# Local attention with scores, transposes and values at the head of a slot; shifted values by transfers; value bias added at the output

## The chip, the core and the metric

The kernel runs on one core of a Trainium2 chip as one program of 63,082 instructions. The core has TensorE (PE, matrix products, and PEld, its weight loads), VectorE (DVE), ScalarE (ACT), GpSimd (POOL) and SyncE (SP), which here only issues transfers. Each engine runs its own instructions in the order in which they were written and waits on semaphores for the others. The metric is the device time of one execution in microseconds; less is better.

## The reference, cut to what matters

A chain of eleven kinds of layer acts on a residual stream of 2048 tokens by 128 channels. Three of them are touched.

```python
# _L1_ffn_ref: two layers, called twice in the network; WINDOW = 64, HEADS = 8, DIM_HEAD = 64, n = 1024, b = 2
def _layer(x, wqkv, qs, ksc, wo, lg, lb, w1, b1, w2, b2):
    q, k, v = jnp.split(shift_token(x) @ wqkv, 3, axis=-1)      # then split into heads
    q, k = rotary_xpos(l2norm(q) * qs, l2norm(k) * ksc)
    o = local_attention(q, k, v)
    x = x + o @ wo
    h = layernorm(shift_token(x)) * lg + lb
    a, g = jnp.split(h @ w1 + b1, 2, axis=-1)
    return x + (a * jax.nn.gelu(g, approximate=False)) @ w2 + b2

def local_attention(q, k, v):            # a window sees itself and the window before
    bk, bv = look_around(bk), look_around(bv)
    sim = jnp.einsum('bhwid,bhwjd->bhwij', bq, bk)
    mask = (i < j) | (i > j + WINDOW) | (j == -1)
    attn = jax.nn.softmax(jnp.where(mask, -jnp.finfo(sim.dtype).max, sim), axis=-1)
    return jnp.einsum('bhwij,bhwjd->bhwid', attn, bv)

# _L1_attn_b_ref (16 heads) and _L2_attn_a_ref (one head, causal)
v = x @ Wv.T + bv
probs = softmax(scores)                  # every row of it sums to 1
out = probs @ v
return out @ Wo.T + bo
```

## The kernel before

`PLAN` lists the stages; `L1f0` and `L1f1` are the two layers of the local-attention block and are run as one stage, twice in the program. Channels lie on the partitions, tokens along the free axis. `PS` is PSUM, eight banks of 128x512; `AR` is the working memory, `WS` the weights, `TP` eight slots of 128x512, `VXT` the shifted values.

**The stage of local attention** (`l1f_pe`, `l1f_act`, `l1f_dve`, `l1f_pool`, `l1f_sp`) is written as a row of 158 slots. The work is cut into 8 groups (a quarter of the tokens in one of the two layers) and each group into 16 units: one pair of heads and 128 queries, that is two windows. Unit `u` is spread over slots: its scores stand in TensorE's slot `u`, the masked maximum (L1986) and the bias for the exponential in VectorE's slot `u`, the two exponentials (L1922) in ScalarE's slot `u`, the reciprocal of the sums (L1994) in VectorE's slot `u+1`, the normalising multiply (L2068) in GpSimd's slot `u+1`. The transposes of the probabilities (L1897) stand in TensorE's slot `u+2`, VectorE's copy of the transposed tile out of PSUM (L2040) too, and the products with the values (L1851, L1853) in TensorE's slot `u+4`. After four units ScalarE copies the output bank 3 (`copy(e, OB[:, r, :], bank(3))`, L518).

Around that, a table (`l1f_dense`) deals the dense work of the next group and of the layer's second half to the slots: `a` (a projection of q or k, read by VectorE for the cosine half, by ScalarE for the raw copy that is swapped), `norm`, `v`, `wide`, `wo`, `ln`, `gate`, `up`, `down`. A slot has a list `first` and a list `second` of them. A dense product of 128x512 in f32 shows as two MATMUL records. TensorE's slot before is: scores, values, `first`, transposes, `second`. VectorE's slot is: masked maximum, bias, reciprocal, dense work of earlier slots, gating of `first`, copy of the transposed tile, gating of `second`, shifted values. Scores have a single pair of banks, so the scores of slot `u+1` wait for the masked maximum of `u`; the transposed tile has a single bank too.

**Shifted values** (`VX`, tile VXT). A window's lower half of keys is its own, the upper half is the window before. So for each of the four tiles of 128 tokens in a group VectorE copies partitions 0 to 63 of that tile (L2047) and 64 to 127 of the tile before (L2049), in slots 1 to 4 of the group.

**SP's queue in this stage** (`l1f_sp`, L2104): the rotary part needs halves of 32 partitions swapped; eight times a group, four transfers of 32x512 go from `RAW` to `TP`. The weights of the stage after next are loaded ahead of the swaps of group 7.

**Value projections.** In `attn16_pe` (stages `L0b`, `L1b`, `L3f`) and in `l2a_pe` (stage `L2a`) 16 products of 128x128 make the values. In `L1b` and `L2a` each is followed by a product with one row of ones and one row of bias (`PS<-WS,CS`, 1x128). The scores' operands of the 16-head stages are brought into place by transfers, 12 of them issued by ScalarE (L1114).

Of the kernel before, what the change touches and what calls it, by code (L numbers as in the profile page):

```python
# [121 lines left out]
def layout(sec, i):  # L122
# [52 lines left out]
    if sec in ("L1b", "L2a"):  # L175
# [3 lines left out]
                ("wo", 128, lambda: i[p + "Wo"].T), ("bv", 128, lambda: rows(i[p + "bv"][None, :])),  # L179
                ("bq", 1, lambda: col(i[p + "bq"][o])), ("bk", 1, lambda: col(i[p + "bk"][o])), ("bo", 1, lambda: col(i[p + "bo"]))]  # L180
# [77 lines left out]
LINES = ("w_in0", "w_in1", "swap_in0", "swap_in1", "swap_in2", "swap_in3", "qk_in0", "qk_in1", "qk_in2", "qk_first", "pad_in", "x_in", "consts_in", "out_done")  # L258
# [190 lines left out]
def program(nc, plan, wall, half, pad, xin, out):  # L449
    where, _ = places(plan)  # L450
    ctx = ExitStack()
    with ctx:
# [20 lines left out]
        swap_in = [F.swap_in0, F.swap_in1, F.swap_in2, F.swap_in3]  # L473
        qk_in = [F.qk_in0, F.qk_in1, F.qk_in2]
# [595 lines left out]
        def ring(k):  # L1070
            return k % 3
# [142 lines left out]
        def attention_act(e, w, s, scale, causal):  # L1214
            units = units_of[causal]
            for kind, n, *args in order[causal]:
# [28 lines left out]
                if kind == "turn":  # L1245
                    c = args[0]
                    w.wait_ge(*F.at_turned.on((s, c)))
                    copy(e, ATTT[:, cs(c)], bank(ring(n))).then_inc(*F.at_out.up((s, c)))
# [80 lines left out]
        def project_v_pe(e, w, s, n, ready, W, bname, heads, banks):  # L1329
            for i in range(16):  # L1330
# [3 lines left out]
                more = [(C("ONE")[0:1, :], W(bname)[0:1, :])] if bname else []  # L1334
                mm(e, bank(b, 8 * heads), (n[:, ts_(i)], W("wv")), *more).then_inc(*F.v_mm.up((s, i)))
# [25 lines left out]
        def l0b_pe(e, w, s, W):  # L1361
# [11 lines left out]
            project_v_pe(e, w, s, n, normal(s), W, None, 4, OWN8)  # L1373
            attention_pe(e, w, s, V4, lambda h: 9 * (h // 4), False, W("wo"), x_added(s))

        def l0b_act(e, w, s, W):
# [5 lines left out]
            attention_act(e, w, s, float(np.float32(128.0) ** np.float32(-0.5)), False)  # L1382
# [29 lines left out]
        def attn16_pe(e, w, s, W, n, ready, causal, bv, added):  # L1412
# [6 lines left out]
            project_v_pe(e, w, s, n, ready, W, bv, 16, OWN8)  # L1419
            attention_pe(e, w, s, V16, lambda h: 9 * h, causal, W("wo"), added)  # L1420

        def attn16_act(e, w, s, W, causal, biased):
# [5 lines left out]
            attention_act(e, w, s, float(8.0 ** -0.5), causal)  # L1428
# [16 lines left out]
        def l1b_pe(e, w, s, W):  # L1445
            attn16_pe(e, w, s, W, big(0), normal(s), False, "bv", x_added(s))
# [320 lines left out]
        def l1f_pe(e, w, s, W0):  # L1767
# [94 lines left out]
            for u in SLOTS:  # L1862
# [16 lines left out]
                if 0 <= u - 4 < UNITS:  # L1879
                    g, r, i = unit(u - 4)  # L1880
                    w.wait_ge(*F.win_pt.on((s, u - 4)))
                    if i == 0:
                        w.wait_ge(*F.head_v_copied.on((s, g, 3)))
                        w.wait_ge(*free[3])
# [1199 lines left out]
```

## Time and profile before

| | |
|---|---|
| three runs | 4466.93, 4472.2, 4471.73 us; median 4471.73 |
| profiled execution | 4480.15 us, span 4478.3 us |
| PE busy | 3922.5 us, 88% of the span |
| DVE busy | 3042.6 us, 68% |
| ACT busy | 2359.4 us, 53% |
| POOL busy | 1224.9 us, 27% |
| mean granted clock of TensorE | 0.909 of 2.4 GHz |

The span goes from the first to the last instruction. Busy shares are averages over the whole program and say little about one stage. "Idle before, releaser" is the time in which an engine stood still ahead of an instruction, and the instruction that released it. The view of waits sums that by pairs: who waited for whom. The chain of waits goes back from the last instruction, at each step to what released it.

### The profile page before, as it was taken

What the parts mean: (1) busy time and instruction counts of PE and PEld (TensorE: products, weight loads), DVE (VectorE), ACT (ScalarE), POOL (GpSimd) and SP (SyncE); (2) the same over time, 40 slices, a digit from 0 to 9 for tenths busy, and PEclk for the clock granted to TensorE, in tenths of its full rate; (3) what the DMA queues carried; (4) which work ended last, traced back from release to release, by engine and by line L of the source; (5) the groups of instructions that cost most, each with busy time, mean ns of one, the idle gap of its engine ahead of it and who ended that gap; (6) DMA issues with size and microseconds to landing.
All of it is one profiled execution on the core that took longest, in us unless ns stands there. A gap on an engine that the chain in (4) does not pass through costs nothing.

```text
span 4478.3 us, 63082 instructions
## 1 busy us (share of the span) xinstructions
PE 3922.5 (88%) x22638; PEld 1897.2 (42%) x22640; DVE 3042.6 (68%) x7970; ACT 2359.4 (53%) x4061; POOL 1224.9 (27%) x1835
## 2 busy tenths in 40 slices
PE   8899968998899988898886778899998999969999
PEld 5222345555432235555552324555554334433343
DVE  4899566878589968877345994566666883278732
ACT  3477644555447765555345553445443673326732
POOL 1100023333220013333112663111113233442334
PEclk8799978889879998988797998899997999979999
DMA  1100002111020011111000000000010100011000
GB/s 55 26 18 16 15 34 72 39 34 42 6 61 20 16 49 43 35 38 28 5 7 5 1 0 9 10 16 17 9 40 20 30 16 1 0 51 28 16 1 10
DMA packets 48336, 104.86 MB, mean 23 GB/s; under 512 B 15220, under 2 KB 15220, under 8 KB 46744
## 3 DMA queue, kind: packets, MB, share of 16 engines
q1 hardware_dynamic: 46872, 99.26, 8.1%
q8 instruction: 179, 2.93, 0.3%
q10 hardware_dynamic: 1152, 1.57, 0.2%
q14 instruction: 133, 1.09, 0.1%
HBM read 41.01 MB, written 1.05 MB: 9 GB/s over the span
## 4 chain that ended last, share of the span: by engine, by line
PE 54%; DVE 29%; ACT 7%; POOL 4%; issue 4%; DMA 1%; ACTq 1%; SPq 0%; POOLq 0%; DVEq 0%
PE PS L511 32%; DVE SM L1274 7%; PE PS L1184 7%; PE PS L1136 5%; PE PS L2743 3%; DVE AR L2547 3%; DVE AR L515 2%; PE PS L1166 2%; DVE AR L1986 1%; PE PS L538 1%; ACT PS L2491 1%; POOL SV L608 1%; ACT AR L518 1%; DVE TP L515 1%; DVE AR L596 1%
## 5 line engine op out<-in xcount | busy, mean ns | idle before, releaser
L511 PE MATMUL PS<-AR,WS 128*128 128x512 f32 (+1 forms) x2112 | 1068.8, 646 | 78.1 <-DVE AR L515 29.6
L1236 ACT ACTIVATE AR<-PS 128x1024 f32<-128x1024 f32 (+3 forms) x896 | 788.9, 931 | 206.0 <-PE PS L1166 201.7
L1274 DVE TENSOR_REDUCE SM<-PS 128x1 f32<-128x512 f32 x1280 | 803.7, 684 | 71.3 <-PE PS L1136 70.3
L518 ACT ACTIVATE AR<-PS 128x512 f32<-128x512 f32 (+6 forms) x600 | 368.7, 623 | 533.9 <-PE PS L511 410.1
L511 PEld LDWEIGHTS PS<-AR,WS 128*128 128x128 f32 (+1 forms) x2112 | 407.9, 204 | 546.8 <-issue 415.4
L1136 PE MATMUL PS<-AR 51*128 51x512 bf16 (+3 forms) x1792 | 508.2, 384 | 61.1 <-DVE SM L1274 16.2
L1184 PE MATMUL PS<-AR 128*32 128x512 f32 (+3 forms) x3584 | 447.6, 572 | 2.5 <-POOL AR L1326 1.9
L1922 ACT ACTIVATE AR<-AR,SM 128x128 f32<-128x128 f32 x512 | 248.3, 486 | 362.3 <-DVE SM L515 360.5
L1136 PEld LDWEIGHTS PS<-AR 51*128 51x128 bf16 x1792 | 133.2, 94 | 597.1 <-DVE SM L1274 407.4
L511 PE MATMUL PS<-AR,H 115*115 115x128 bf16 (+3 forms) x912 | 212.3, 311 | 104.4 <-DVE TP L2550 37.5
L2068 POOL TENSOR_TENSOR AR<-AR,SM 128x256 f32<-128x256 f32 x256 | 162.9, 636 | 486.9 <-DVE SM L1994 473.4
L1166 PE MATMUL PS<-AR 51*128 51x512 bf16 (+3 forms) x1792 | 288.7, 366 | 8.3 <-ACT AR L1236 5.3
L2817 DVE TENSOR_TENSOR AR<-AR,PS 128x512 f32<-128x512 f32 x128 | 87.5, 688 | 256.7 <-PE PS L511 256.7
L1312 POOL CAST MBT<-SM 128x8 bf16<-128x8 f32 x128 | 28.2, 221 | 840.6 <-DVE SM L1277 699.3
L606 POOL TENSOR_SCALAR SV<-LNS 128x4 f32<-128x4 f32 x148 | 28.8, 195 | 834.8 <-DVE LNS L589 563.8
L1271 DVE CUSTOM_DVE_ANT_0 TP<-PS,H 128x384 f32<-128x384 f32 (+3 forms) x512 | 226.3, 487 | 41.3 <-PE PS L1136 35.8
L515 DVE SCALAR_TENSOR_TENSOR AR<-PS,WS,AR 128x512 f32<-128x512 f32 x148 | 109.7, 748 | 186.2 <-PE PS L511 155.6
L511 PE MATMUL PS<-AR 128*128 128x16 f32 (+3 forms) x920 | 198.0, 366 | 27.9 <-DVE AR L913 10.9
L2831 POOL TENSOR_TENSOR AR<-AR 128x512 f32<-128x512 f32 x128 | 159.4, 1268 | 228.8 <-ACT AR L518 228.8
L511 PE MATMUL PS<-WS,AR 128*128 128x256 f32 (+4 forms) x640 | 205.6, 456 | 15.3 <-DVE TP L515 6.0
L511 PEld LDWEIGHTS PS<-AR,H 115*115 115x115 bf16 (+3 forms) x912 | 98.9, 121 | 272.4 <-DVE TP L2550 60.7
L2075 POOL TENSOR_TENSOR AR<-AR,TP 128x512 f32<-128x512 f32 x128 | 162.2, 1267 | 142.5 <-DVE TP L515 142.5
(320 smaller groups left out, 6969.4 us busy)
## 6 DMA issues: line engine op xcount, KB each, us to landing
TP<-RAW SPq DMA_DIRECT2D x512, 64.0 KB, 2.0
AR<-AR SPq DMA_DIRECT2D x720, 32.0 KB
WS<-wall SPq DMA_DIRECT2D x4, 3654.5 KB, 11.2
WS<-wall SPq DMA_DIRECT2D x8, 902.5 KB, 4.5
WS<-wall SPq DMA_DIRECT2D x2, 3334.5 KB, 11.0
WS<-wall SPq DMA_DIRECT2D x1, 2384.0 KB, 9.1
WS<-wall SPq DMA_DIRECT2D x1, 1543.5 KB, 6.2
AR<-AR ACTq DMA_DIRECT2D x48, 32.0 KB
```

The lines of the kernel that those rows point to most:

```text
L511: t = e.matmul(o, l, r, start=(n == 0), stop=(n == len(pairs) - 1))
L515: return e.scalar_tensor_tensor(out=o, in0=a, scalar=s, in1=b, op0=f1, op1=f2)
L518: return e.activation(o, i, ACT.Copy, scale=1.0)
L1136: e.matmul(bank(p, m), l, r, start=True, stop=True).then_inc(*F.at_scores_max.up((s, k, i, rr, k0, g)))
L1166: t = e.matmul(sv[:, g, off:512], l, r, start=True, stop=True)
L1184: t = e.matmul(bank(7)[32 * j:32 * j + 32, t0:t1], V[:, 8 * b + kti, v0:v0 + 32], pv[:, j % 2, t0:t1], start=(kti == 0), stop=(kti == nk - 1))
L1236: e.activation(pv[:, :, off:512], sv[:, :, off:512], ACT.Exp, scale=scale).then_inc(*F.at_exp.up((s, u, p2)))
L1271: e.tensor_tensor_reduce(out=slot(5 + len(masked) % 3, m), in0=bank(ring(n + g), m), in1=H["MASKED"][:, 512 - m:512], scale=1.0, scalar=-3 ...
L1274: e.tensor_reduce(top, bank(ring(n + g), m), AX.X, ALU.max).then_inc(*F.at_max.up((s, k, i, rr, k0, g)))
L1922: t = e.activation(pw[:, z, :], pw[:, z, :], ACT.Exp, bias=nm[:, 2 + z:3 + z], scale=rq[:, z:z + 1], accum_out=nm[:, 4 + z:5 + z])
L2068: e.tensor_tensor(pw, pw, nm[:, 4:6].unsqueeze(2).to_broadcast([128, 2, 128]), ALU.mult).then_inc(*F.win_p.up((s, u - 1)))
L2075: e.tensor_tensor(d, d, slot(4 + j % 4), ALU.add).then_inc(*F.head_sum.up((s, g, j)))
```

## The change

1. In TensorE's slot the transposes move from behind `first` to right behind the scores, ahead of the values. Both dense lists follow.
2. In VectorE's slot the copy of the transposed tile moves to right behind the bias, ahead of the reciprocal.
3. In ScalarE's slot the copy of the output bank moves ahead of the exponentials.
4. The shifted values are no longer copied by VectorE but transferred, by SP, with four semaphores of their own. In SP's queue the swaps of a group now go one group ahead, and the transfers of shifted values stand between the first four of them.
5. In `L1b` and `L2a` the bias of the values is not multiplied into every value but added when the attention's output is copied out of PSUM (the weights of a row sum to 1). The bias is kept as one column instead of 128.

```diff
@@ l1f_pe
                     scores(u).then_inc(*F.win_score.up((s, u)))
+                if 0 <= u - 2 < UNITS:
+                    w.wait_ge(*F.win_p.on((s, u - 2)))
+                    w.wait_ge(*(F.win_pt.on((s, u - 3)) if u >= 3 else free[2]))
+                    for g in range(2):
+                        t = e.transpose(TURNED[:, g, :], pw[:, g, :], C("I"))
+                    t.then_inc(*F.win_turned.up((s, u - 2)))
                 if 0 <= u - 4 < UNITS:
                     w.wait_ge(*F.win_pt.on((s, u - 4)))
-                    w.wait_ge(*F.win_vx.on((s, g, i)))
+                    w.wait_ge(*vx_in[i].on((s, g, i)))
                     values(u - 4).then_inc(*F.win_pv.up((s, u - 4)))
                 dense(first)
-                if 0 <= u - 2 < UNITS:
...
                 dense(second)
@@ l1f_act
+                if 0 <= u - 4 < UNITS and u % 4 == 3:
+                    w.wait_ge(*F.win_pv.on((s, u - 4)))
+                    copy(e, OB[:, r, :], bank(3)).then_inc(*F.win_o.up((s, g, r)))
                 if 0 <= u < UNITS:
                     for z in range(2):
                         t = e.activation(pw[:, z, :], pw[:, z, :], ACT.Exp, bias=nm[:, 2 + z:3 + z], scale=rq[:, z:z + 1], accum_out=nm[:, 4 + z:5 + z])
-                if 0 <= u - 4 < UNITS and u % 4 == 3:
...
@@ l1f_dve
                     stt(e, nm[:, 2:4], nm[:, 0:2], -1.0, rq, ALU.mult, ALU.mult).then_inc(*F.win_bias.up((s, u)))
+                if 0 <= u - 2 < UNITS:
+                    w.wait_ge(*F.win_turned.on((s, u - 2)))
+                    e.tensor_copy(PTR[(u - 2) % 3], TURNED).then_inc(*F.win_pt.up((s, u - 2)))
...
-                if 0 <= u < UNITS and 1 <= u % 16 <= 4:
-                    t = e.tensor_copy(VX[0:64, i, :], VH[0:64, 4 * (g % 2) + i, :])
-                    if i or g % 2:
-                        t = e.tensor_copy(VX[64:128, i, :], VH[64:128, 4 * (g % 2) + i - 1, :])
@@ l1f_sp
+            def shifted_values(g, i):
+                w.wait_ge(*F.head_v_copied.on((s, g, 3)))
+                if g:
+                    w.wait_ge(*F.win_pv.on((s, 16 * g - 4 + i)))
+                e.dma_start(VX[0:64, i, :], VH[0:64, 4 * (g % 2) + i, :]).then_inc(*vx_in[i].up((s, g, i), 16))
+                if i or g % 2:
+                    last = (4 * (g % 2) + i - 1) % 8
+                    e.dma_start(VX[64:128, i, :], VH[64:128, last, :]).then_inc(*vx_in[i].up((s, g, i), 16))
+            for j in range(8):
+                swap(0, j)
             for g in range(8):
-                if g == 7:
+                if g == 6:
                     load(e, s + 2)
                 for j in range(8):
+                    if j < 4:
+                        shifted_values(g, j)
+                    if g < 7:
+                        swap(g + 1, j)
@@ project_v_pe, and alike in l2a_pe
-                more = [(C("ONE")[0:1, :], W(bname)[0:1, :])] if bname else []
-                mm(e, bank(b, 8 * heads), (n[:, ts_(i)], W("wv")), *more).then_inc(*F.v_mm.up((s, i)))
+                mm(e, bank(b, 8 * heads), (n[:, ts_(i)], W("wv"))).then_inc(*F.v_mm.up((s, i)))
@@ attention_act (bv is 0.0 where a stage has no bias), and alike in l2a_act
-                    copy(e, ATTT[:, cs(c)], bank(ring(n))).then_inc(*F.at_out.up((s, c)))
+                    e.activation(ATTT[:, cs(c)], bank(ring(n)), ACT.Identity, bias=bv).then_inc(*F.at_out.up((s, c)))
```

TensorE, first pass of local attention, slot 2 of the third group. L1838, L1840 and L1842 are the scores, L1851 and L1853 the values, L1897 the transposes, L511 dense work. Before:

```order
L1838 MATMUL PS<-AR 64x64 [waits win_dve]
L1838 MATMUL PS<-AR 64x64
L1840 MATMUL PS<-AR 64x128 x2
L1842 MATMUL PS<-AR 64x64 x2
L1851 MATMUL PS<-AR 64x64 x2
L1853 MATMUL PS<-AR,VXT 64x64 x2
L511 MATMUL PS<-AR,WS 128x512 [waits head_act]
L1897 MATMUL PS<-CS,AR 128x128 [waits win_dve,win_pool]
L1897 MATMUL PS<-CS,AR 128x128
L511 MATMUL PS<-CS,TP 128x2 [waits ln_act,head_act]
L511 MATMUL PS<-CS,TP 128x2 x3
```

After (L1884 are the transposes, L512 the dense work):

```order
L1838 MATMUL PS<-AR 64x64 [waits win_dve]
L1838 MATMUL PS<-AR 64x64
L1840 MATMUL PS<-AR 64x128 x2
L1842 MATMUL PS<-AR 64x64 x2
L1884 MATMUL PS<-CS,AR 128x128 [waits win_dve,win_pool]
L1884 MATMUL PS<-CS,AR 128x128
L1851 MATMUL PS<-AR 64x64 x2
L1853 MATMUL PS<-AR,VXT 64x64 x2
L512 MATMUL PS<-AR,WS 128x512 [waits head_act]
L512 MATMUL PS<-CS,TP 128x2 [waits ln_act,head_act]
L512 MATMUL PS<-CS,TP 128x2 x3
```

The transposes and their wait for VectorE and GpSimd have moved ahead of the values and of the 128x512 product; nothing stands between the two dense lists any more.

VectorE, slot 2 of the same group. L1986 is the masked maximum, L515 with SM the bias, L1994 the reciprocal, L2040 the copy of the transposed tile, L2047 and L2049 the shifted values. Before:

```order
L1986 ISA AR,SM<-PS,H 128x128 [waits win_pe]
L1986 ISA SM 128x1
L1986 ISA AR,SM<-PS,H 128x128
L1986 ISA SM 128x1
L515 SCALAR_TENSOR_TENSOR SM<-SM 128x2 [waits win_dve]
L1994 RECIPROCAL SM<-SM 128x2 [waits win_act]
L515 SCALAR_TENSOR_TENSOR AR<-PS,WS 128x512 [waits head_act]
L515 SCALAR_TENSOR_TENSOR TP<-TP,WS 128x512 [waits swap_in0]
L2040 COPY AR<-PS 128x256 [waits win_pe]
L2047 COPY VXT<-AR 64x512
L2049 COPY VXT<-AR 64x512
```

After (L1995 is the copy of the transposed tile, L1999 the reciprocal, L516 the rest):

```order
L1986 ISA AR,SM<-PS,H 128x128 [waits win_pe]
L1986 ISA SM 128x1
L1986 ISA AR,SM<-PS,H 128x128
L1986 ISA SM 128x1
L516 SCALAR_TENSOR_TENSOR SM<-SM 128x2 [waits win_dve]
L1995 COPY AR<-PS 128x256 [waits win_pe]
L1999 RECIPROCAL SM<-SM 128x2 [waits win_act]
L516 SCALAR_TENSOR_TENSOR AR<-PS,WS 128x512 [waits head_act]
L516 SCALAR_TENSOR_TENSOR TP<-TP,WS 128x512 [waits swap_in0]
```

The copy, with its wait for TensorE, stands ahead of the reciprocal and of the dense work; both copies into VXT are gone.

SP, the first slots of the second group of the first pass, after. L2090 is a swap, L2096 and L2099 are the shifted values:

```order
L2096 DMA VXT<-AR 64x512 [waits win_pe,head_act]
L2099 DMA VXT<-AR 64x512
L2090 DMA TP<-RAW 32x512 [waits head_pool,head_act]
L2090 DMA TP<-RAW 32x512 x3
L2096 DMA VXT<-AR 64x512 [waits win_pe]
L2099 DMA VXT<-AR 64x512
L2090 DMA TP<-RAW 32x512 [waits head_pool,head_act]
L2090 DMA TP<-RAW 32x512 x3
```

Before, the swaps stood alone there. Now a wait for TensorE's values (win_pe) stands ahead of each of the first four swaps.

## Rows read from the trace of the kernel before

**Rows 1.** The page, the chain that ended last, by engine.

```profile
PE 54%; DVE 29%; ACT 7%; POOL 4%; issue 4%; DMA 1%; ACTq 1%; SPq 0%; POOLq 0%; DVEq 0%
```

**Rows 2.** Busy times in both passes: us, busy (records) by engine, clock, DMA, GB/s.

```profile
737.00:1215.00 478.00, 425.06 (x3740) 255.64 (x3738) 365.96 (x1425) 264.61 (x744) 164.66 (x205) 0.89 0.14 33
1693.00:2165.00 472.00, 414.19 (x3722) 251.04 (x3721) 362.87 (x1413) 262.35 (x741) 164.06 (x204) 0.89 0.14 33
```

**Rows 3.** TensorE's waits, first pass: who for whom, total us, times, longest.

```profile
PE PS L1851 <- ACT AR L518: 13.5, 12, 2.0
PE PS L1838 <- DVE SM L1986: 12.8, 22, 1.5
PE PS L1897 <- DVE AR L2040: 8.3, 14, 1.1
```

**Rows 4.** TensorE's waits, second pass.

```profile
PE PS L1851 <- ACT AR L518: 15.7, 16, 2.0
PE PS L1897 <- DVE AR L2040: 15.1, 22, 2.9
PE PS L1838 <- DVE SM L1986: 10.2, 19, 0.7
```

**Rows 5.** Groups by line: busy us, mean ns, idle before and its releasers.

```profile
L2040 DVE COPY AR<-PS 128x256 f32<-128x256 f32 x256 | 106.7, 417 | 84.3 <-PE PS L1897 83.7
...
L1897 PEld LDWEIGHTS PS<-CS,AR 128*128 128x128 f32 x512 | 66.0, 150 | 127.8 <-issue 105.6 <-POOL AR L2068 17.7
...
L2047 DVE COPY VXT<-AR 64x512 f32<-64x512 f32 x64 | 57.4, 898 | 0.0
```

**Rows 6.** Timeline 900.9 to 901.4, TensorE: start us, length us, line, shapes, records.

```profile
901.03 0.20 PEld L1897 LDWEIGHTS PS<-CS,AR 128*128 128x128 f32 x2
901.03 0.44 PE L1897 MATMUL PS<-CS,AR 128*128 128x128 f32 x2
```

**Rows 7.** Timeline 908 to 911, all engines.

```profile
908.18 0.38 PE L1897 MATMUL PS<-CS,AR 128*128 128x128 f32 x2
...
908.50 0.27 PE L1838 MATMUL PS<-AR 64*64 64x64 f32 x2
...
908.72 0.23 PE L1842 MATMUL PS<-AR 64*64 64x64 f32 x2
...
908.87 0.34 PE L1851 MATMUL PS<-AR 128*64 128x64 f32 x4
908.94 0.41 DVE L2047 COPY VXT<-AR 64x512 f32<-64x512 f32 x1
...
909.79 0.14 PEld L1897 LDWEIGHTS PS<-CS,AR 128*128 128x128 f32 x1 [0.24 <-issue]
909.82 0.29 DVE L1986 CUSTOM_DVE_ANT_0 AR<-PS,H 128x128 f32<-128x128 f32 x1
...
910.22 0.38 PE L1897 MATMUL PS<-CS,AR 128*128 128x128 f32 x2
...
910.44 0.73 PE L511 MATMUL PS<-CS,TP 128*128 128x2 f32 x6
...
910.68 0.61 POOL L2068 TENSOR_TENSOR AR<-AR,SM 128x256 f32<-128x256 f32 x1 [2.53 <-DVE SM L1994]
```

**Rows 8.** SP's issues of the swaps by source line.

```profile
L2104 SPq DMA_DIRECT2D TP<-RAW x512: 507/591/2063, 704.3 to 2090.2; - x171
...
DMA to landing us min/median/max: 1.9/2.0/3.8
```

**Rows 9.** Value projections: the one-row products by line.

```profile
L511 PE MATMUL PS<-WS,CS 1*128 1x128 f32 x64 | 22.4, 444 | 0.0
```

**Rows 10.** Timeline at the end of the value projection, 16 heads, TensorE.

```profile
1267.26 1.03 PE L1136 MATMUL PS<-AR 51*128 51x512 bf16 x3
```

**Rows 11.** Timeline of ScalarE's transfers there.

```profile
1249.30 9.09 ACTq L1114 DMA_DIRECT2D AR<-AR  x12
```

**Rows 12.** Timeline at the first score of the single-head stage.

```profile
2222.89 0.80 PE L2135 MATMUL PS<-AR 128*128 128x128 f32 x2 [0.37 <-ACT AR L518]
```

More of the change, by code:

```diff
@@ L1410, in program, with attn16_pe @@
         SIDES = [("wq", "bq", QP), ("wk", "bk", KP)]
-        def attn16_pe(e, w, s, W, n, ready, causal, bv, added):
+        def attn16_pe(e, w, s, W, n, ready, causal, added):
             for j in range(8):
@@ L1445, in l1b_pe @@
         def l1b_pe(e, w, s, W):
[L1446 removed]
+            attn16_pe(e, w, s, W, big(0), normal(s), False, x_added(s))
         def l1b_act(e, w, s, W):
@@ L1898, in l1f_pe @@
                     t.then_inc(*F.win_turned.up((s, u - 2)))
+                if 0 <= u - 4 < UNITS:
+                    g, r, i = unit(u - 4)
+                    w.wait_ge(*F.win_pt.on((s, u - 4)))
+                    if i == 0:
+                        w.wait_ge(*F.head_v_copied.on((s, g, 3)))
+                        w.wait_ge(*free[3])
+                    w.wait_ge(*vx_in[i].on((s, g, i)))
+                    values(u - 4).then_inc(*F.win_pv.up((s, u - 4)))
+                if 0 <= u - 4 < UNITS:
+                    g, r, i = unit(u - 4)
+                    if i == 3:
+                        free[3] = F.win_o.on((s, g, r))
+                dense(first)
                 if u == -2:
@@ L2092, in l1f_sp, with swap @@
         def l1f_sp(e, w, s):
+            def swap(g, j):
+                done, into = swap_in[j % 4], slot(4 + j % 4)
+                w.wait_ge(*F.head_raw.on((s, g, j)))
+                if 8 * g + j >= 4:
+                    w.wait_ge(*F.head_sum.on((s, g, j - 4) if j >= 4 else (s, g - 1, j + 4)))
+                for p in range(4):
+                    e.dma_start(into[32 * p:32 * p + 32, :], RAW[j % 2][32 * (p ^ 1):32 * (p ^ 1) + 32, :]).then_inc(*done.up((s, g, j), 16))
+            def shifted_values(g, i):
+                w.wait_ge(*F.head_v_copied.on((s, g, 3)))
+                if g:
[6 more added lines that the diff above has]
+                swap(0, j)
             for g in range(8):
-                if g == 7:
+                if g == 6:
                     for c in ALL:
@@ L2183, in l2a_act @@
                     w.wait_ge(*F.one_pv.on((s, u - 2)))
-                    copy(e, n[:, ts_(8 * b + i)], bank(6 + u % 2, 128)).then_inc(*F.one_out.up((s, u - 2)))
+                    e.activation(n[:, ts_(8 * b + i)], bank(6 + u % 2, 128), ACT.Identity, bias=W("bv")).then_inc(*F.one_out.up((s, u - 2)))
         def l2a_dve(e, w, s, W):
```

62 lines of the change are left out of this document (18 added, 44 removed).

## The prediction

> **What bounds the kernel now.** I read the chain of waits first: TensorE holds 54% of the span, VectorE 29%, ScalarE 7% [rows 1]. So no engine alone sets the end; the loop through several of them does in places. The change sits in two stages, local attention (which the plan runs twice) and the two value projections with a bias, so the busy times of the local-attention passes come next: 478 and 472 us long, TensorE busy 425.1 and 414.2, VectorE 366.0 and 362.9, granted clock 0.89 in both [rows 2]. TensorE sits idle for 53 + 58 = 111 us in them, and that is the most that any reordering of waits can give back. Who ends those waits is in the view of waits. In the first pass: values waiting for ScalarE's copy of the output bank 13.5 us, scores waiting for VectorE's masked maximum 12.8, transposes waiting for VectorE's copy of the transposed tile 8.3 [rows 3]. In the second: 15.7, 10.2 and 15.1 [rows 4]. Together 29.2 for the output bank, 23.0 for the maximum, 23.4 for the transposed copy: 75.6 of the 111 us.
>
> VectorE is late for two visible reasons. It shifts the values itself, 57.4 us in 64 copies of the lower half and 56 more of the upper half, and in the slot shown a pair of them, begun at 908.94, stands ahead of the masked maximum that begins at 909.82, though the scores had ended at 908.72 + 0.23 = 908.95 [rows 5, 7]. And it stands idle 84.3 us ahead of the copy of the transposed tile, 83.7 of them for TensorE, because the transposes come behind a dense product [rows 5].
>
> **The change, part by part.** My profiled execution took 4480.15 us (span 4478.3), the median shown is 4471.73; I work on the profiled one and move the difference to the median.
>
> *Waits of TensorE that go.* With ScalarE's output copy ahead of its exponentials, the bank is asked for a slot later than it is freed: the 29.2 us go. With VectorE's copy at the head of its slot, transposes no longer meet it: the 23.4 go. Of the 23.0 for the maximum I take 16: VectorE loses the shifting copies (57.4 and, at this slot's 0.41 for each of the 56 others, 23, so 80 us) and most of 84 us idle, against 729 busy [rows 2, 5, 7]; what stays late are slots in which its own dense work is long. Sum -69. Bounds: -52 if the maximum's waits all stay, -76 if all three go. What is late next is the product chain of TensorE itself.
>
> *What the head order costs TensorE.* Today a pair of transposes between two dense products costs 0.22 us (start 910.22 to the next start 910.44), and its weight load runs from 909.79 under the product before it. Behind the scores it has no such cover: where transposes follow the small value products, load and product start together at 901.03, and the pair takes 0.44 instead of 0.38 us; where scores follow transposes, 908.18 to 908.50, it is 0.32 [rows 6, 7]. From scores to values is 0.15 today (908.72 to 908.87). The new head has two such changes of tile where there was one: 0.15 + 0.32 against 0.15 + 0.22 at least, so +0.10, and +0.2 if the step behind the scores is as long as the longer ones. I take 0.15 in each of the 256 slots, +38 us (26 to 51). This is TensorE's own time, nothing hides it where TensorE is the bound. The Trainium skill ("TensorE: Matmul & The Clock Gate", section "Step-by-step: what each phase is for") says that TensorE pulls weight loads ahead of matmuls in flight, when row groups don't conflict or the load goes to the background buffer. By that rule a load is free behind a long product, and there the trace agrees (0.43 us ahead in 909.79 to 910.22); if it held behind the scores too the term would be near 0 and the sum 38 us lower, but the 901.03 rows show no lead.
>
> *A new wait.* The transposes now stand at the head of TensorE's queue behind their wait for the probabilities, and values and dense products behind them. The normalising multiply on GpSimd ends 1.47 us after the masked maximum begins (909.82 to 910.68 + 0.61); VectorE's copy of the transposed tile now stands between, +0.42, so 1.89. A slot with one dense product and nothing more lasts 0.37 (908.50 to 908.87) + 1.35 (values and product, to 910.22) + 0.32 (transposes, as above) = 2.04 us [rows 7]. From scores ended at 0.45 in one slot, the probabilities are ready at 0.45 + 0.08 + 1.89 = 2.42; the transposes want them at 2.04 + 0.37 = 2.41, or 0.15 later with the dearer head. So on time they cost nothing, and each microsecond by which VectorE is late in a short slot is paid on TensorE. Even now 17.7 us of weight loads of transposes wait for GpSimd, with a product ahead of most [rows 5]. Bounds: 0, and 17.7 plus one product of 0.96 for about as many loads as there are short slots in which VectorE's own dense work is longest (two in 16, so 32): 48. I take 15, nearer to the low end since VectorE sheds over 100 us; that is one late microsecond per 16 slots.
>
> *Shifted values by transfer.* 120 more issues in SP's queue. One swap issue takes 591 ns in the median, and landing 2.0 us [rows 8]. In four slots of every 16 SP now issues 2 + 4 = 6 transfers, 3.5 us, in slots of 2 to 3.5 us, so it falls behind by a few us, and the fifth slot has no issue and holds the output projection, four products. The shifted values are wanted four slots after they are issued. I take 0; if the swaps' readers on VectorE do wait, up to 2.4 us (one swap) in each of 16 groups, +38. The early load of the next stage's weights stands where it stood, between the swaps of group 6 and those of group 7.
>
> *Bias out of the value projection.* 64 records of one-row products, 22.4 us busy, half in each of two stages [rows 9]. In the 16-head attention the last pair of them stands right ahead of the scores, which start at 1267.26. Without them the scores are held by the transfers that ScalarE issues until 1249.30 + 9.09 = 1258.39 and their landing 2.0 later, so they can start at 1260.4: -6.9 us [rows 8, 10, 11]. In the single-head stage the first score starts at 2222.89, 0.37 us after TensorE ran out of work, held by the copy of the last product; nothing else is in the way, so half of the busy time, 11.2, less what overlaps, -10.4 [rows 12]. Bounds for both together: -14 and -20. ScalarE's copies of the attention's output become copies with a bias, 16 wide ones and 16 narrow ones; no row separates what that adds, I take +1.5 us for the 32 (0 to 3, a tenth of a microsecond each at most where nothing hides it). The weights that shrink by 127 columns load long before they are used: 0.
>
> Sum: -69 + 38 + 15 + 0 - 17.3 + 1.5 = -32, that is 4448 for the profiled execution and 4439 against the median of 4471.73.
>
> **Rivals** (times against the median of 4471.73). (1) *The loop was the bound.* VectorE sheds 80 us of copies and 84 us of idling, and if the remaining waits of TensorE fall with it (the 111 us down to some 15) and transposes are never late: -96 + 38 - 16 = -74, 4398. For it: 29% of the chain on VectorE [rows 1]. Against it: TensorE is already busy 88% of the passes.
> (2) *Local attention gives nothing.* The new wait and the switches eat the 69: -16 from the bias alone, 4456. For it: 38 + 31 is inside the bounds above.
> (3) *Slower.* VectorE now waits for the transposes with its reciprocal, sines, norms and gating behind, the transposes wait for GpSimd, and GpSimd for that reciprocal one slot earlier. Each late slot is then handed on instead of being absorbed behind the first dense product. If half of the 256 slots are late by one product's worth, 0.96 us: +123 - 69 + 38 - 16 = +76, 4548; at 0.6 us +40, 4512. It decides from 47 us of new waits on. Against it: the one-product slot just meets, and by the table that places the dense work only four or five slots in 16 are that short.
> (4) *SP's queue.* Swaps late by one swap in each group: -32 + 38 = +6, 4478. For it: the four issues of a swap alone fill 2.4 us of a slot [rows 8]. Against it: the wide fifth slot.
>
> **How the numbers follow.** About 0.2% of the median, 9 us, is what a measurement can tell. Forecast 0.46 (own range 4422 to 4455), rival 1 0.18, rival 2 0.17, rival 3 0.13, rival 4 0.06. Faster by over 0.2% (below 4463): the forecast but for 0.02, rival 1, and half of rival 2, 0.71. Within: the rest of rival 2 and most of rival 4, 0.15. Slower: 0.14. The range that leaves two in ten outside reaches from 4402, into rival 1, to 4480, past rivals 2 and 4; rival 3 stays out. The granted clock of 0.89 in the passes is left where it is: fewer gaps may raise it, and more short products at the head may lower it; both ends are inside the range.
>
> **What would show it.** Waits of values for ScalarE's copy and of transposes for VectorE's copy near 0; VectorE's idle time ahead of that copy far under 84 us; a wait of the transposes on GpSimd that stands on TensorE itself, about 15 us in both passes; 0.3 us between transposes and values in each slot; scores of the 16-head stage held by a transfer; passes shorter by 8 us each. The prediction is wrong if that GpSimd wait passes 47 us, if VectorE waits for swaps by more than 20 us, or if TensorE's idle time in the passes falls below 30 us.

## The result and the profile after

| | before | after |
|---|---|---|
| median of the timed runs, us | 4471.97 (4466.93 to 4476.41, 4 runs) | 4451.24 (4446.88 to 4454.48, 4 runs) |
| ratio after/before, 95% interval | | 0.9953 [0.9936, 0.9971] |
| profiled execution, us (its span) | 4480.15 (4478.3) | 4450.58 (4448.7) |

The change gains 21 us by the medians and 30 between the two profiled executions. The prediction said 4439, with a range of 4402 to 4480. The time lies in the forecast's own range (4422 to 4455), but the traces tell a different story from the one forecast: nearly all of the gain comes from the bias, and local attention gave back what it won.

The page after has the chain that ended last by engine [rows 1]: VectorE's share went down by three points and TensorE's went up by as many.

```profile
PE 57%; DVE 26%; ACT 6%; POOL 5%; issue 4%; SPq 1%; DMA 1%; ACTq 0%; POOLq 0%; DVEq 0%
```

From mark to mark, after against before: each pass of local attention from its first scores to its last values, +2.8 and -5.5 us; from there to the first score of the 16-head stage -6.4, of the single-head stage -18.6; everything else together -1.9. Sum -29.6, the difference of the spans.

Busy times in both passes, after. The columns are those of rows 2, but the windows here end with the last values of a pass:

```profile
736.00:1202.00 466.00, 432.37 (x3709) 253.36 (x3710) 337.93 (x1350) 264.85 (x740) 164.33 (x204) 0.86 0.22 50
1688.00:2147.00 459.00, 429.84 (x3711) 253.43 (x3710) 338.19 (x1350) 264.64 (x740) 164.35 (x204) 0.86 0.22 51
```

The same stretches before (in rows 2 some us more stood behind the last values):

```profile
738.00:1200.00 462.00, 410.12 (x3708) 249.22 (x3700) 360.59 (x1410) 260.30 (x739) 164.58 (x204) 0.89 0.15 34
1693.00:2157.00 464.00, 406.68 (x3710) 247.72 (x3708) 361.75 (x1411) 260.14 (x739) 164.06 (x204) 0.90 0.14 34
```

926 us became 925. TensorE's idle time fell as meant, from 109.2 to 62.8 us. Its busy time rose by the same amount, from 816.8 to 862.2, for the same number of products. And the granted clock fell from 0.89 to 0.86.

TensorE's waits after, first pass [rows 3] and second pass [rows 4]:

```profile
PE PS L1884 <- POOL AR L2059: 22.5, 32, 1.6
PE PS L1838 <- DVE SM L1986: 7.3, 14, 0.8
...
PE PS L1884 <- POOL AR L2059: 19.6, 29, 1.6
PE PS L1838 <- DVE SM L1986: 6.2, 11, 0.8
```

The waits for the output copy (29.2) and the transposed copy (23.4) are gone, as forecast. 13.5 of 23.0 us for the masked maximum stay, and transposes now wait 42.1 us for GpSimd's multiply.

One slot of TensorE after, at the full clock (start, length): scores, transposes, values [rows 7].

```profile
968.69 0.23 PE L1842 MATMUL PS<-AR 64*64 64x64 f32 x2
968.85 0.44 PE L1884 MATMUL PS<-CS,AR 128*128 128x128 f32 x2
969.22 0.34 PE L1851 MATMUL PS<-AR 128*64 128x64 f32 x4
```

The transposes take 0.37 us from start to start of what follows, where they took 0.22 between dense products.

VectorE's side, after: its copy by line [rows 5], and its waits in the first pass.

```profile
L1995 DVE COPY AR<-PS x256: 410/417/425, 740.6 to 2143.6; 128x256 f32<-128x256 f32 x128
its engine sat idle before it (us, times) until:
  PE PS L1884: 4.2, 12
```

```profile
DVE AR L1986 <- PE PS L1842: 64.3, 58, 5.2
DVE AR L516 <- PE PS L512: 26.7, 16, 3.8
DVE TP L516 <- DMA TP<-RAW: 15.4, 16, 2.1
```

84.3 us of idling ahead of the copy became 4.2, but VectorE now idles 64.3 us in this pass (66.3 in the second) for scores: it is the follower. It waits 15.4 + 14.7 us for swaps, against 3.5 + 7.4 before.

The start of the 16-head scores [rows 10] and the value projection of the single-head stage with its first score [rows 12], after:

```profile
1261.97 0.97 PE L1137 MATMUL PS<-AR 51*128 51x512 bf16 x3 [2.85 <-DMA AR<-AR]
...
2189.59 3.73 PE L512 MATMUL PS<-WS,AR 128*128 128x128 f32 x32
2193.69 0.49 PE L2143 MATMUL PS<-AR 128*128 128x128 f32 x2 [0.37 <-ACT AR L519]
```

### The profile page after: what moved, and what is told of

It reads as the page before. It is cut to its first block, busy times and chain, and to the rows that moved or that the text cites. A ratio compares the mean times of both kernels' runs of the same rounds, so it can differ in the third digit from the quotient of the medians.

```text
span 4448.7 us, 62998 instructions
## 1 busy us (share of the span) xinstructions
PE 3930.3 (88%) x22576; PEld 1885.0 (42%) x22576; DVE 2994.7 (67%) x7850; ACT 2368.0 (53%) x4061; POOL 1223.3 (27%) x1835
## 4 chain that ended last, share of the span: by engine, by line
PE 57%; DVE 26%; ACT 6%; POOL 5%; issue 4%; SPq 1%; DMA 1%; ACTq 0%; POOLq 0%; DVEq 0%
PE PS L512 32%; DVE SM L1275 7%; PE PS L1185 7%; PE PS L1137 5%; DVE AR L2555 3%; PE PS L2751 3%; DVE AR L516 2%; PE PS L1167 2%; PE PS L1884 2%; PE PS L539 1%; ACT PS L2499 1%; POOL SV L609 1%; DVE SV L516 1%; PE PS L1851 1%; DVE AR L1986 1%
## 5 line engine op out<-in xcount | busy, mean ns | idle before, releaser
L512 PE MATMUL PS<-AR,WS 128*128 128x512 f32 (+1 forms) x2112 | 1062.3, 643 | 68.4 <-DVE AR L516 26.1
L519 ACT ACTIVATE AR<-PS 128x512 f32<-128x512 f32 (+6 forms) x568 | 358.9, 637 | 571.7 <-PE PS L512 403.0
L512 PEld LDWEIGHTS PS<-AR,WS 128*128 128x128 f32 (+1 forms) x2112 | 405.6, 203 | 524.3 <-issue 411.9
L1137 PE MATMUL PS<-AR 51*128 51x512 bf16 (+3 forms) x1792 | 507.1, 382 | 63.6 <-DVE SM L1275 16.2
L512 PE MATMUL PS<-AR,H 115*115 115x128 bf16 (+3 forms) x912 | 208.4, 310 | 104.3 <-DVE TP L2558 37.5
L516 DVE SCALAR_TENSOR_TENSOR AR<-PS,WS,AR 128x512 f32<-128x512 f32 x148 | 109.7, 748 | 198.0 <-PE PS L512 181.4
L512 PE MATMUL PS<-WS,AR 128*128 128x256 f32 (+4 forms) x640 | 207.6, 466 | 18.6 <-DVE TP L516 8.6
L512 PE MATMUL PS<-AR 128*128 128x16 f32 (+3 forms) x920 | 193.0, 360 | 27.9 <-DVE AR L914 10.9
L1986 DVE CUSTOM_DVE_ANT_0 AR<-PS,H 128x128 f32<-128x128 f32 x512 | 127.7, 287 | 133.1 <-PE PS L1842 130.6
L512 PEld LDWEIGHTS PS<-AR,H 115*115 115x115 bf16 (+3 forms) x912 | 97.8, 121 | 268.8 <-DVE TP L2558 60.7
## 6 DMA issues: line engine op xcount, KB each, us to landing
WS<-wall SPq DMA_DIRECT2D x2, 3334.5 KB, 10.4
```

Of the source, the lines that this page charges most:

```text
L512: t = e.matmul(o, l, r, start=(n == 0), stop=(n == len(pairs) - 1))
L516: return e.scalar_tensor_tensor(out=o, in0=a, scalar=s, in1=b, op0=f1, op1=f2)
L519: return e.activation(o, i, ACT.Copy, scale=1.0)
L1137: e.matmul(bank(p, m), l, r, start=True, stop=True).then_inc(*F.at_scores_max.up((s, k, i, rr, k0, g)))
L1986: t = e.tensor_tensor_reduce(out=PW[u % 4][:, z, :], in0=bank(z, 128), in1=H["BAND0" if top(u) else "BAND"], scale=1.0, scalar=-3.0e38, op ...
```

## The experiments

The parts are numbered as in the change: 1 TensorE's order, 2 VectorE's order, 3 ScalarE's copy, 4 shifted values, 5 bias. Each ratio is to the kernel before, run on the same chip.

| run | parts | median us | ratio, 95% interval |
|---|---|---|---|
| e1 | 5 | 4452.10 | 0.9945 [0.9930, 0.9960] |
| e2 | 1 2 3 4 | 4469.27 | 0.9989 [0.9974, 1.0003] |
| e3 | none, bias products of 128 rows | 4454.31 | 0.9950 [0.9938, 0.9962] |
| e4 | 3 | 4442.83 | 0.9918 [0.9905, 0.9932] |
| e5 | 4 | 4431.12 | 0.9907 [0.9890, 0.9924] |
| e6 | 1 2 | 4476.41 | 1.0012 [0.9996, 1.0029] |
| e7 | 3 4 5 | 4389.83 | 0.9816 [0.9797, 0.9834] |
| e8 | 3 5 | 4417.13 | 0.9875 [0.9857, 0.9893] |
| e9 | all, transposes behind values, reciprocal first | 4396.44 | 0.9831 [0.9812, 0.9849] |
| e10 | all, reciprocal first | 4418.76 | 0.9882 [0.9867, 0.9896] |
| e11 | 1 3 4 5 | 4449.41 | 0.9946 [0.9929, 0.9962] |
| e12 | all, and one needless product a slot | 4418.04 | 0.9882 [0.9866, 0.9899] |

### Bias and local attention apart

e1 is the kernel before with part 5 alone:

```diff
-                mm(e, bank(b, 8 * heads), (n[:, ts_(i)], W("wv")), *more).then_inc(*F.v_mm.up((s, i)))
+                mm(e, bank(b, 8 * heads), (n[:, ts_(i)], W("wv"))).then_inc(*F.v_mm.up((s, i)))
...
-                    copy(e, ATTT[:, cs(c)], bank(ring(n))).then_inc(*F.at_out.up((s, c)))
+                    e.activation(ATTT[:, cs(c)], bank(ring(n)), ACT.Identity, bias=bv).then_inc(*F.at_out.up((s, c)))
```

e2 is the changed kernel with these hunks undone.

> The kernel before with the value bias added at the output alone (part 5); local attention as before. Theory A (the value projections carry nearly all of the gain): 20 to 25 us less than before, about 4449, as both stages' first scores moved by 6.4 and 18.6 us between the two traces. Rival B (both parts share the gain, and 10 us of the 18.6 are a clock state that the shorter local attention left behind): 12 to 15 us less, and the value products of the single-head stage fall to 1.2 GHz on their way.

> The changed kernel with the one-row bias products put back (parts 1 to 4 alone). Theory A: within 6 us of before, since TensorE's idle time in the passes fell by 48 us and its busy time rose by 39. Rival B: 10 us or more below before.

The bias alone is worth 25 us, more than the 16 of the sum (theory A of e1). Local attention as a whole is not told apart from nothing: its interval runs from -12 to +1 us.

e3 leaves everything as before, but the product that adds the bias takes all 128 rows (127 of them zero) in place of one:

```diff
-                more = [(C("ONE")[0:1, :], W(bname)[0:1, :])] if bname else []
+                more = [(C("ONE"), W(bname))] if bname else []
...
-                mm(e, bank(k, 128), (n[:, ts_(i)], W("wv")), (C("ONE")[0:1, :], W("bv")[0:1, :])).then_inc(*F.one_v.up((s, i)))
+                mm(e, bank(k, 128), (n[:, ts_(i)], W("wv")), (C("ONE"), W("bv"))).then_inc(*F.one_v.up((s, i)))
```

> The kernel before, its bias products with all 128 rows (ones by a matrix whose first row is the bias, the rest zeros): as many products and bytes of result, the same sum, no change of the number of rows between two products. If a one-row product costs what it does because the number of rows changes at each (0.42 us a product against 0.23 in the changed kernel), the single-head value phase shrinks from 20 to about 7.5 us and the kernel by 15 to 20 us. If every product has its own fixed cost, it stays within 5 us of before.

It gains 22 us, nearly as much as leaving the products out. In the single-head value projection before, two adjoining lines near its start, and two later:

```profile
2203.31 0.49 PE L511 MATMUL PS<-WS,AR 128*128 128x128 f32 x2
2203.73 0.48 PE L511 MATMUL PS<-WS,CS 1*128 1x128 f32 x2
...
2216.66 0.80 PE L511 MATMUL PS<-WS,AR 128*128 128x128 f32 x2
2217.39 0.79 PE L511 MATMUL PS<-WS,CS 1*128 1x128 f32 x2
```

The same place with 128 rows:

```profile
2192.08 0.39 PE L511 MATMUL PS<-WS,AR 128*128 128x128 f32 x2
...
2198.33 0.39 PE L511 MATMUL PS<-WS,AR 128*128 128x128 f32 x2
2198.55 0.39 PE L511 MATMUL PS<-WS,CS 128*128 128x128 f32 x2
```

From start to start a line takes 0.42 us where one row and 128 rows alternate, then 0.72 after 2207; 0.22 throughout where all have 128. The second step is the clock. Over the whole value projection before, the window row is

```profile
2202.60:2222.90 20.30, 19.93 (x66) 13.72 (x64) 0.00 (x0) 5.13 (x19) 0.00 (x0) 0.60 0.00 0
```

with TensorE busy 19.93 of 20.30 us and a granted clock of 0.60, most of it at 1.2 GHz. The value products themselves cost half of the 19.93 us; by the sum I had left them as they were. Without the bias products the 16 tiles take 3.73 us, in e1 as in the changed kernel, and the first score comes 4.1 us after the first of them where it came 20.3 after: 16.2 of the 18.6 us. The other 2.4 lie ahead of the value projection.

### The parts of local attention, one by one

e4, e5 and e6 are the kernel before with one edit each. e4, ScalarE's slot:

```diff
+                    copy(e, OB[:, r, :], bank(3)).then_inc(*F.win_o.up((s, g, r)))
                     for z in range(2):
                         t = e.activation(pw[:, z, :], pw[:, z, :], ACT.Exp, bias=nm[:, 2 + z:3 + z], scale=rq[:, z:z + 1], accum_out=nm[:, 4 + z:5 + z])
-                    copy(e, OB[:, r, :], bank(3)).then_inc(*F.win_o.up((s, g, r)))
```

e5, VectorE's slot and SP's queue, the swaps a group ahead as in the change:

```diff
-                    t = e.tensor_copy(VX[0:64, i, :], VH[0:64, 4 * (g % 2) + i, :])
...
+                e.dma_start(VX[0:64, i, :], VH[0:64, 4 * (g % 2) + i, :]).then_inc(*vx_in[i].up((s, g, i), 16))
```

e6, TensorE's slot and VectorE's:

```diff
                     scores(u).then_inc(*F.win_score.up((s, u)))
+                        t = e.transpose(TURNED[:, g, :], pw[:, g, :], C("I"))
                     values(u - 4).then_inc(*F.win_pv.up((s, u - 4)))
                 dense(first)
-                        t = e.transpose(TURNED[:, g, :], pw[:, g, :], C("I"))
...
+                    e.tensor_copy(PTR[(u - 2) % 3], TURNED).then_inc(*F.win_pt.up((s, u - 2)))
                     e.reciprocal(nm[:, 4:6], nm[:, 4:6]).then_inc(*F.win_recip.up((s, u - 1)))
                 gated(first)
-                    e.tensor_copy(PTR[(u - 2) % 3], TURNED).then_inc(*F.win_pt.up((s, u - 2)))
```

e7 is the changed kernel with this edit of e6 undone, and e8 the kernel before with the edits of e1 and e4.

> The kernel before with ScalarE's copy of the output bank ahead of the exponentials alone (part 3). My prediction's step: TensorE's 29 us of waits of the values for that copy go, and the kernel falls by up to 29 us if nothing takes their place. Rival: they are handed to the next wait of VectorE's slot (masked maximum, transposed copy), which is late in the same slots, and under 10 us are left.

> The kernel before with the shifted values by SP's transfers alone (part 4). Theory A (VectorE's 80 us of copies stand on the path in the slots where it is late): 8 to 15 us below before, with the scores' waits for the masked maximum halved. Rival B (the transfers cost what they free: swaps queue behind them and VectorE's and ScalarE's waits for swaps, 11 and 3 us in the passes before, rise): within 6 us of before.

> The kernel before with the head order on TensorE and VectorE alone (parts 1 and 2). Theory A (the copy of the output bank is what gains in local attention, the head order loses what is missing): 15 to 35 us above before. Rival B (the head order is neutral, and the loss comes from its meeting the transfers): within 8 us of before.

> The changed kernel with the order of before on TensorE and VectorE (parts 3, 4 and 5 stay). Theory A: the sum of its parts, 25 (bias) + 35 (output copy) + what e5 shows, so 60 us or more below before and 35 to 45 below the changed kernel; the wait of transposes for GpSimd on TensorE falls from 42 us to under 10. Rival B (the output copy's gain and the head order's are the same microseconds): within 10 us of the changed kernel.

> The kernel before with parts 3 and 5 alone: ScalarE's output copy first, bias at the output. They lie in different stages, so if both stand by themselves the gains add: 25 + 35 = 60 us below before, about 4415. If the shorter value phases only shifted the clock's low stretches, 40 to 45.

By the ratios the copy alone is worth 37 us and the transfer 42, both more than was expected of them, and the copy adds up with the bias (e8: -56 where e1 and e4 make -62). All three together don't: 25 + 37 + 42 = 104, and e7 has 82. The head order alone is neutral. On top of the other parts it costs 61 us: e7 is at 4389.83, the changed kernel at 4451.24. In e4 the 29 us of waits for the output copy are gone, but the transposes wait 31.8 us for VectorE's copy where they waited 23.4. In e5 the scores' waits for the masked maximum fell from 23.0 to 15.5 us, not by half. e5 moves the swaps a group ahead as well as the copies to transfers, and no run parts the two. The windows of e4, e5, e6 and e7 (their passes from first scores to last values) show more:

```profile
738.00:1181.00 443.00, 399.82 (x3711) 246.40 (x3710) 365.71 (x1410) 261.59 (x740) 164.09 (x204) 0.90 0.15 35
1673.00:2118.00 445.00, 401.09 (x3710) 246.54 (x3708) 366.17 (x1410) 260.70 (x739) 164.10 (x204) 0.90 0.15 35
```

```profile
740.00:1178.00 438.00, 390.75 (x3708) 240.92 (x3708) 330.44 (x1350) 260.71 (x739) 163.73 (x204) 0.93 0.23 54
1673.00:2108.00 435.00, 387.61 (x3697) 239.21 (x3697) 329.33 (x1350) 261.19 (x740) 164.13 (x204) 0.94 0.23 54
```

```profile
737.00:1197.00 460.00, 418.26 (x3711) 246.80 (x3710) 373.50 (x1410) 263.09 (x740) 167.51 (x204) 0.89 0.15 34
1689.00:2154.00 465.00, 422.57 (x3712) 246.71 (x3709) 373.26 (x1410) 263.16 (x740) 167.45 (x204) 0.89 0.14 34
```

```profile
739.00:1166.00 427.00, 386.44 (x3709) 240.12 (x3710) 328.47 (x1351) 261.46 (x740) 164.31 (x204) 0.94 0.24 55
1651.00:2086.00 435.00, 394.85 (x3712) 243.78 (x3711) 328.46 (x1350) 261.80 (x740) 163.75 (x204) 0.92 0.23 54
```

The time at 1.2 GHz in a window is twice its length times what the clock lacks of 1: for the kernel before 462 x 0.22 + 464 x 0.20 = 194 us. The clock has two digits, so this is good to 9 us, and the last column to 4. TensorE has one order of work in the first four rows, and the head order in the last four (e10 and e11 follow below; they change VectorE's slot alone):

| | passes us | idle | busy | at 1.2 GHz | busy, less what the clock took |
|---|---|---|---|---|---|
| before | 926 | 109 | 817 | 194 | 724 |
| e4 | 888 | 87 | 801 | 178 | 716 |
| e5 | 873 | 95 | 778 | 113 | 724 |
| e7 | 862 | 81 | 781 | 121 | 723 |
| e6 | 925 | 84 | 841 | 203 | 762 |
| after | 925 | 63 | 862 | 259 | 761 |
| e10 | 891 | 71 | 820 | 152 | 761 |
| e11 | 933 | 87 | 846 | 215 | 762 |

The last column takes off 0.48 of the time at 1.2 GHz in the old order and 0.39 in the head order. Each factor is read from the two ends of its group: 38 us of busy time for 81 at the lower clock (before and e5), 42 for 107 (after and e10). The other rows fall in line within 8 us in the old order and within 1 in the head order. Why the factors differ is not shown; one part of it may be that a pair of transposes at the head stretches less at 1.2 GHz (0.62 us to the values for 0.37) than one between dense products did (0.48 for 0.22).

Against before, rows alone tell it. The head order by itself (e6) adds 24 us of busy time at the same clock and takes away 25 of idle time. With copy and transfers too, another 21 us of idle time go, and at 0.86 instead of 0.89 the same order of work takes 21 us more: -1 in all. Against e7 the changed kernel has 81 us more busy time, 54 by the clock (0.39 x 138) and 27 by the head order, and 18 less idle time: +63.

### Is it the wait, the tile changes or the clock?

These four start from the changed kernel. e10 swaps two instructions of VectorE:

```diff
                     stt(e, nm[:, 2:4], nm[:, 0:2], -1.0, rq, ALU.mult, ALU.mult).then_inc(*F.win_bias.up((s, u)))
+                    e.reciprocal(nm[:, 4:6], nm[:, 4:6]).then_inc(*F.win_recip.up((s, u - 1)))
                     e.tensor_copy(PTR[(u - 2) % 3], TURNED).then_inc(*F.win_pt.up((s, u - 2)))
-                    e.reciprocal(nm[:, 4:6], nm[:, 4:6]).then_inc(*F.win_recip.up((s, u - 1)))
```

e9 does that too and puts the transposes behind the values:

```diff
                     scores(u).then_inc(*F.win_score.up((s, u)))
-                        t = e.transpose(TURNED[:, g, :], pw[:, g, :], C("I"))
                     values(u - 4).then_inc(*F.win_pv.up((s, u - 4)))
+                        t = e.transpose(TURNED[:, g, :], pw[:, g, :], C("I"))
                 dense(first)
```

e11 keeps TensorE's order and undoes VectorE's:

```diff
-                    e.tensor_copy(PTR[(u - 2) % 3], TURNED).then_inc(*F.win_pt.up((s, u - 2)))
                     e.reciprocal(nm[:, 4:6], nm[:, 4:6]).then_inc(*F.win_recip.up((s, u - 1)))
                 gated(first)
+                    e.tensor_copy(PTR[(u - 2) % 3], TURNED).then_inc(*F.win_pt.up((s, u - 2)))
```

e12 adds a product:

```diff
-                    w.wait_ge(*F.win_p.on((s, u - 2)))
                     w.wait_ge(*(F.win_pt.on((s, u - 3)) if u >= 3 else free[2]))
+                    e.matmul(bank(2), H["I"], H16[:, 0:512], start=True, stop=True)
+                    w.wait_ge(*F.win_p.on((s, u - 2)))
                     for g in range(2):
                         t = e.transpose(TURNED[:, g, :], pw[:, g, :], C("I"))
```

> The changed kernel with TensorE's head in the order scores, values, transposes, dense products, and VectorE's reciprocal ahead of its copy of the transposed tile. The transposes come about 1 us later than in the changed kernel, the multiply on GpSimd 0.4 us earlier. Theory A (the new wait on GpSimd, 42 us, and the lower clock that goes with it are most of the 61 us by which the changed kernel lies behind the same kernel with the old head order): the wait falls under 10 us, the time to 4395 to 4410. Rival B (the changes of tile, 0.15 us in each of 256 slots, are most of it): the two small groups in one row are still there, so the time stays within 15 us of 4451, at 4435 to 4450.

> The changed kernel with VectorE's reciprocal ahead of its copy of the transposed tile, nothing else. The multiply on GpSimd can begin 0.4 us earlier; TensorE's order stays. Theory A: of the 42 us of waits on GpSimd, in 61 slots, some 20 go and the clock gains as much again: 4410 to 4430. Rival B: 20 us at most, since the tile changes stay and values then wait for the later copy: 4440 to 4455.

> The changed kernel with VectorE's copy of the transposed tile back behind its first gated work, and only TensorE's transposes at the head of the slot. Theory A: GpSimd's multiply starts 0.4 us earlier as in the run before, but the copy that frees the bank for the next transposes comes later, so a wait on VectorE's copy takes the place of the one on GpSimd: 4425 to 4450. Rival C (it is VectorE's half of the head order that costs, by standing idle for the transposes): near the kernel with the old order, 4390 to 4405.

> The changed kernel with one needless bf16 product of 128x512 added on TensorE in each of the 256 slots, between scores and transposes, ahead of the wait for GpSimd. It takes about 0.22 us at the full clock: 56 us if nothing hides it; some 15 us of it lie in the waits on GpSimd. Theory D (the low clock is a cause by itself: 270 us of the two passes run at half clock, against 123 us with the old head order, worth about 45 us): the clock of the passes rises from 0.86 to above 0.92 and pays the product back, so the time comes out within 20 us of 4451. Rival: the clock only follows from other waits; it stays near 0.86 and the time is 4490 to 4510.

Waits of e10 and then of e12, first and second pass each:

```profile
PE PS L1884 <- POOL AR L2059: 19.1, 35, 2.0
...
PE PS L1884 <- POOL AR L2059: 21.4, 38, 2.0
```

```profile
PE PS L1885 <- POOL AR L2060: 23.1, 47, 1.4
...
PE PS L1885 <- POOL AR L2060: 22.2, 44, 1.4
```

The windows of e10, of e9, of e12 and of e11:

```profile
737.00:1185.00 448.00, 415.43 (x3703) 245.60 (x3696) 334.49 (x1350) 263.50 (x739) 161.41 (x204) 0.90 0.22 52
1672.00:2115.00 443.00, 404.37 (x3709) 239.35 (x3709) 333.97 (x1350) 262.36 (x740) 161.38 (x204) 0.93 0.23 53
```

```profile
739.00:1170.00 431.00, 392.85 (x3709) 238.55 (x3708) 339.36 (x1351) 260.25 (x739) 161.42 (x204) 0.92 0.23 54
1658.00:2095.00 437.00, 401.12 (x3710) 241.82 (x3708) 338.43 (x1350) 260.71 (x739) 161.41 (x204) 0.90 0.23 53
```

```profile
735.00:1184.00 449.00, 407.91 (x3777) 245.49 (x3836) 337.78 (x1351) 262.57 (x739) 164.02 (x204) 0.97 0.22 52
1669.00:2113.00 444.00, 403.59 (x3777) 242.97 (x3838) 336.48 (x1351) 262.92 (x740) 164.37 (x204) 0.98 0.23 53
```

```profile
736.00:1200.00 464.00, 417.72 (x3711) 245.00 (x3710) 330.29 (x1350) 264.54 (x740) 164.23 (x204) 0.90 0.22 50
1685.00:2154.00 469.00, 428.31 (x3710) 249.36 (x3708) 329.95 (x1350) 265.15 (x739) 164.20 (x204) 0.87 0.21 50
```

e12 shows that the clock is a cause by itself. TensorE does 256 products more than in the changed kernel and waits for GpSimd as long (45.3 us against 42.1). Yet the kernel is 33 us faster, at a granted clock of 0.97 and 0.98 against 0.86. The gain isn't in the idle time, which is 81 us against 63; of those 81, 11.5 are needless products without a record in the trace (122 of the 256 lack one). It is in the busy time, 51 us shorter, or some 40 with the products that lack a record. Not all of that is clock, though. One slot of e12 at the full clock:

```profile
966.69 0.39 PE L1882 MATMUL PS<-H 128*128 128x512 bf16 x1
966.92 0.38 PE L1885 MATMUL PS<-CS,AR 128*128 128x128 f32 x2
967.23 0.34 PE L1851 MATMUL PS<-AR 128*64 128x64 f32 x4
```

Behind the needless product the transposes take 0.31 us to the values where they took 0.37, some 14 us over the slots. So the added work is 256 x 0.23 less 14, about 45 us. The table's measure agrees: 811.5 - 0.39 x 45 = 794, with the 11.5 us without a record 805, 44 more than the 761 of after. The clock paid 0.39 x 214 = 83 for them. Theory D had asked for a clock above 0.92 and a time within 20 us; the clock is higher and the gain greater.

e10 fell in theory A's range, but not for its reason. The wait on GpSimd stayed, at 40.5 us. Its clock in the passes is 0.90 and 0.93; 891 us of passes less 820 busy leave 71 idle, 8 more than in the changed kernel, and the busy time is 42 us less, for the same order of work on TensorE. So theory A holds only by half: the clock is what gained, and the wait is not what made the changed kernel slow. e6 says the same from the other side: its transposes wait 54.0 us for GpSimd, and its clock is 0.89.

e9 took the wait on GpSimd down to 10.5 us and came within 7 us of e7, with a clock of 0.92 and 0.90. Rival B's time is refuted, but not the cost it names, since e9 takes part of that away too:

```profile
968.53 0.44 PE L1896 MATMUL PS<-CS,AR 128*128 128x128 f32 x2
968.80 1.02 PE L512 MATMUL PS<-AR,WS 128*128 128x512 f32 x2
```

Ahead of a dense product the pair takes 0.27 us where it takes 0.37 ahead of the values, some 21 us over the slots in which it stands so. e9 changes wait, clock and places at once, and doesn't weigh them singly.

e11's rows show the other half of the pair. VectorE's late copy holds the transposes at the head:

```profile
PE PS L1884 <- DVE AR L2040: 41.7, 46, 2.0
...
PE PS L1884 <- DVE AR L2040: 36.5, 42, 2.1
```

78.2 us of waits on VectorE took the place of the 42.1 on GpSimd, as theory A said, and the clock was again better, 0.90 and 0.87; together no change that can be told (4449 against 4451). Rival C is refuted.

## Why the prediction was right, and where its steps were not

The time was right because errors cancelled. What happened in local attention is the course of rival 2, the new wait and the dearer work eat what the waits give back, which I gave 0.17; its 4456 is only 5 us from the result. The sum had -16 us there (-69 + 38 + 15) and the passes gave -2.7.

- *Waits that go, -69.* Right for two of three: 29.2 and 23.4 went. Of the masked maximum 9.5 went where I took 16.
- *Head order, +38.* The single step is right: 0.37 against 0.22 us, 0.15 more. But in 86 of the 256 slots the transposes of before had no dense product behind them, and ahead of scores they took 0.31 to 0.37 already (908.18 to 908.50 in [rows 7]); there the move adds little. Summed over the slots, by the steps at the full clock, it adds 28 us. e6 shows 24 at a clock of 0.89. The table's 38 at the full clock (761 - 723) is read beyond its rows, and its agreement with the forecast is not evidence for 0.15 in each slot.
- *New wait, +15.* It is the term of the sum that was mis-sized: 42.1 us, near the upper bound of 48. It is 61 waits of 0.7 us each, where I took one of 1 us in every 16 slots.
- *Shifted values, 0.* The waits of VectorE for swaps rose by 19.2 us to 30.1, past the 20 that I had named as a sign of being wrong. No loss came of it that a run shows: the transfers alone, with the swaps moved ahead, are worth 42 us (e5), though VectorE waits 21.0 us for swaps in its first pass. The gain had no term of its own.
- *Bias, -17.3 and +1.5.* The 16-head stage was right: scores held by a transfer, 6.4 us earlier where I had 6.9. The single-head stage gained 18.6 for 10.4, 16.2 of them in the value projection: I priced the one-row products by their own busy time and not the products that alternate with them, nor the clock. No run separates the +1.5 for ScalarE's copies with a bias.
- *The clock, left at 0.89.* This is the step that failed. It fell to 0.86, which costs 21 us (e6 against after), and the prediction had no price for it beyond "both ends are inside the range". It also carries most of what each part is worth alone: of e5's 53 us in the passes 38 are busy time at a better clock, 15 idle time.

That the passes would each be 8 us shorter was wrong (+2.8, -5.5). Rival 3 did not decide: its 47 us of new waits were not reached. Its second figure was added up wrong: half of the slots at 0.6 us make 77 - 69 + 38 - 16 = +30 and 4502, not +40 and 4512. Rival 1 had its size, 4398, in e7 and e9, but not its mechanism: neither has TensorE's idle time below 70 us.

What stays open: why the clock falls with the head order only when copy and transfers are there too (e6 keeps 0.89). The runs show that it does and what it costs, not what starts it. The wait on GpSimd by itself doesn't: it is 54.0 us in e6 and 40.5 in e10, both with a better clock than the changed kernel.

## What to carry to other kernels

Price a reordering of TensorE in three terms and not in one: idle time, busy time at the full clock, and time at the lower clock. A change can take half of the idle time away and give it all back as slower products. Where a change joins several edits, run them singly: here three of the five were worth 82 us and the two with the plainest reason cost 61, so that the version without them (e7, 4389.83 us, 0.9816 [0.9797, 0.9834]) beats both kernels.

## What the hardware showed unexpectedly

A needless product can pay for itself. One bf16 product of 128x512 in each slot of two passes raised the granted clock from 0.86 to 0.97 and made the kernel 33 us faster, 14 of them at most by the shorter step behind it. Whether it would help e7, whose clock is already 0.93, was not tried.

The clock differs between runs of one and the same kernel, and the time with it. In the 12 runs of e2 it lay between 0.901 (span 4482.9 us) and 0.910 (4450.3 us); a line through them falls by 36 us for each 0.01. Much of the spread of this kernel's times goes with it.

It fell without a gap, too. In the single-head value projection before, TensorE was busy 98% of the time and came down to 1.2 GHz in the midst of the alternating products (dense products ran without a break ahead of them, from 2195.71 on), while 128-row products in their place ran at the full clock (0.22 us each to the end). The Trainium skill ("TensorE: Matmul & The Clock Gate", section "HAM oscillation — how this bites in real kernels") puts a falling clock down to stretches in which TensorE sits idle. This trace doesn't bear that out here.

A one-row product is dearer than one with 128 rows among 128-row products: 0.42 us against 0.22 at the full clock, for it and for its neighbour alike. Fewer rows save nothing.
